# Two token groups in the expert stage of a MetaFormer block: scattered rows, plain loads, an early join

## The reference, cut to what matters

```python
x = x + _L0_conv_ref(_ln_c(x), ...)          # spectral filter, 16 images of 16x16 pixels, 128 channels
t = _to_tokens(x)                             # 4096 tokens of 128 features
t = t + _L0_ffn_ref(_ln_t(t), gate_w, w1, w3, w2)

def _L0_ffn_ref(x, gate_w, w1, w3, w2):       # 8 experts, the best 2 per token, hidden size 384
    gate_logits = xf @ gate_w.T
    weights, indices = jax.lax.top_k(gate_logits, TOP_K)
    weights = jax.nn.softmax(weights, axis=-1)
    for e in range(E):
        h = jax.nn.silu(xf @ w1[e].T) * (xf @ w3[e].T)
        y = h @ w2[e].T
        out = out + combine[:, e:e + 1] * y
```

## Time and profile before

| what | us |
|---|---|
| median of 3 runs (lowest to highest) | 434.74 (433.69 to 437.81) |
| profiled execution, its own time | 437.45 |
| its span, first to last instruction | 435.7 |
| busy in the span: PE, DVE, ACT, POOL | 359.9, 228.7, 166.6, 232.8 |

### The profile page before, as it was taken

The page is one execution under the profiler, slowest core; times in us unless marked ns, Lnnn a source line. Parts: engine busy times, 40 slices in busy tenths (PEclk is TensorE's granted clock), DMA queues, the critical chain, the costliest instruction groups (busy, mean ns, idle before and its releaser), DMA issues.

```text
span 435.7 us, 7026 instructions
## 1 busy us (share of the span) xinstructions
PE 359.9 (83%) x2198; PEld 288.6 (66%) x2198; DVE 228.7 (52%) x556; ACT 166.6 (38%) x326; POOL 232.8 (53%) x255
## 2 busy tenths in 40 slices
PE   1999999963999999859946999999999989989500
PEld 0666666322588888745635999988888888878500
DVE  3376544363479999934972444443334334333147
ACT  2445544322132322145303545444334344434146
POOL 3374342434776555410017577777777777777600
PEclk9999999995899999977955999999999999999955
DMA  7950000035212331571001111111111111112178
GB/s 243 268 127 2 2 0 0 2 84 114 56 42 72 92 90 60 182 257 70 0 6 49 38 54 51 55 50 51 53 56 48 53 52 48 56 50 56 47 260 321
DMA packets 16934, 35.04 MB, mean 80 GB/s; under 512 B 4468, under 2 KB 6152, under 8 KB 16392
## 3 DMA queue, kind: packets, MB, share of 16 engines
q1 hardware_dynamic: 11048, 24.94, 18.6%
q0 software_dynamic: 4544, 9.32, 6.8%
q10 hardware_dynamic: 1312, 0.40, 0.6%
HBM read 21.02 MB, written 9.37 MB: 70 GB/s over the span
## 4 chain that ended last, share of the span: by engine, by line
PE 47%; POOL 23%; issue 10%; DMA 9%; DVE 8%; ACT 2%; SPq 1%; ACTq 0%; POOLq 0%; DVEq 0%
POOL shared L597 11%; POOL y_dram L602 11%; PE psum L823 8%; PE psum L1034 6%; PE psum L912 4%; PE psum L804 3%; PE psum L812 3%; PE psum L1018 3%; PE psum L973 3%; PE psum L888 3%; DMA shared<-tn_dram,idx_gather 2%; PE psum L937 2%; DVE xn L1076 2%; DMA rwc<-in_rwc 2%; PE psum L1009 2%
## 5 line engine op out<-in xcount | busy, mean ns | idle before, releaser
L597 POOL DMA_INDIRECT shared<-tn_dram,idx_gather x71 | 69.0, 972 | 58.7 <-DVE idx_gather L1318 37.3
L602 POOL DMA_INDIRECT y_dram<-shared,idx_scatter x71 | 70.1, 987 | 26.2 <-issue 19.8
L754 ACT ACTIVATE shared<-psum 128x384 f32<-128x384 f32 x71 | 34.8, 491 | 51.5 <-PE psum L1034 50.9
L1034 PE MATMUL psum<-RS,xgt_hl 128*128 x142 | 52.4, 369 | 0.7 <-issue 0.6
L1034 PE MATMUL psum<-w_hi,xgt_hl 128*128 x142 | 48.7, 343 | 0.0
L1076 DVE TENSOR_SCALAR xn<-T,mv,rstd 128x128 f32<-128x128 f32 (+1 forms) x64 | 41.5, 734 | 5.4 <-POOL rstd L510 5.4
L1336 DVE COPY shared<-psum 128x256 f32<-128x256 f32 (+1 forms) x36 | 15.2, 421 | 54.8 <-PE psum L1001 49.9
L1034 PE MATMUL psum<-w_lo,xgt_hl 128*128 x142 | 36.9, 341 | 0.0
L749 ACT ACTIVATE xgt_hl<-psum 128x256 fp32r<-128x256 f32 (+1 forms) x36 | 13.7, 381 | 56.4 <-PE psum L1001 56.4
L1329 DVE TENSOR_TENSOR shared<-shared,psum 128x384 f32<-128x384 f32 x36 | 20.0, 554 | 27.5 <-ACT shared L754 27.5
L823 PE MATMUL psum<-xp,sp 128*64 128x256 f32 x288 | 33.7, 388 | 0.0
(11 more groups left out here) (180 smaller groups left out, 731.8 us busy)
## 6 DMA issues: line engine op xcount, KB each, us to landing
star<-y_dram SPq DMA_DIRECT2D x16, 256.0 KB, 5.6
star<-in_w SPq DMA_DIRECT2D x2, 1536.0 KB, 8.9
rw<-spec SPq DMA_DIRECT2D x8, 256.0 KB, 3.5
turned_b<-spec SPq DMA_DIRECT2D x8, 256.0 KB, 3.6
tn_dram<-xn SPq DMA_DIRECT2D x8, 256.0 KB, 2.1
out<-T SPq DMA_DIRECT2D x8, 256.0 KB, 3.4
spec<-in_w SPq DMA_DIRECT2D x1, 1536.0 KB, 6.6
shared<-in_sp_even SPq DMA_DIRECT2D x1, 1280.0 KB, 15.0
```

The costliest lines, as they stand in the source:

```text
L597: pool.indirect_dma_start(xg[j % BUFS], None, tn_dram, bass.IndirectOffsetOnAxis(ap=idx_gather[:, j:j + 1], axis=0)).then_inc(S[f"g_x{j % ...
L602: pool.indirect_dma_start(y_dram, bass.IndirectOffsetOnAxis(ap=idx_scatter[:, j:j + 1], axis=0), yo[:, j % BUFS * P:j % BUFS * P + P], Non ...
L754: act.activation(silu[j % 2], p_h1[j % 2][:, 0:HID], ACT.Silu).then_inc(S["f_silu"], 1)
L1034: mm = pe.matmul(h[:, 0:HID], xgt[j // 2 % 2][xs][:, j % 2 * P:j % 2 * P + P], w_hl[ws][:, cols], start=(n == 0), stop=(n == 2))
```

## The change

The tokens are cut into two groups: pairs 0 to 3 and pairs 4 to 7. Every expert has a region of rows in DRAM for each group, large enough for all tokens of the group (`xs_dram`), so a token's row can be sent there as soon as its place within the expert is known.

- A row has 130 floats: 128 features, the token's number and its best expert. ACT writes it (`normalise_tokens`, in place of DVE's), with a shift and a scale that POOL makes.
- DVE chooses the experts of group 0 in two halves, at the end of steps 3 and 5 (`choose`: the 11 operations of `top_two` and two copies), places them in steps 4 and 6 (`place`) and makes the tables of the loop (`tables`, 15 operations). PE ranks them with f16 matmuls (`rank`: 9, 17 and, for group 1, 17).
- POOL scatters the rows (`dispatch`), two per token tile: 4 in each of steps 4 to 7, 16 after the last step, all group 0; 8 of group 1 before the loop and 2 in each of its steps 2 to 13.
- From step 4 on the spatial products of the next pair (5, 6, 7) are DVE's instead of POOL's. The step loop is written out.
- w1 and w3 are loaded in the second stage; their splits, the last turns and gatings are interleaved.
- The loop has 39 tiles a group, 78 in all, 40 steps. SP loads each tile as one block whose first row it reads from a table (`load`). Pads of 128 rows mark the ends of the regions; those of group 1 are written between the loads of tiles 7 and 8. DVE makes the scatter addresses from the two extra columns (`slots`, two operations a step).
- Group 0's results are loaded in steps 28 and 34 and joined by DVE in steps 27 to 36 (`join`, 4 operations in each of 8 steps); its pairs are stored before the end. The last four pairs are joined as before.

```diff
+GROUPS = 2
+G_PAIRS = PAIRS // GROUPS
+G_TILES = TILES // GROUPS
 BUFS = 8
-STEPS = (RUN_TILES + 1) // 2
+ROW = DIM + 2
+REGION = G_TILES * P + P
+G_ROWS = E * REGION + E * P
+G_RUN = (2 * G_TILES * P + E * (P - 1)) // P
+G_STEPS = (G_RUN + 1) // 2
+G_SLOTS = 2 * G_STEPS
+STEPS = GROUPS * G_STEPS
-GROUPS = 4
-EARLY = 4 * (PAIRS - 3)
+LATE = PAIRS - 3
+PART_LOAD = G_STEPS + 8
+JOIN_AT = (G_STEPS + 7, G_STEPS + 9, G_STEPS + 13, G_STEPS + 15)
...
+            def pads(g):
+                sp.wait_ge(S["q_tables"], g + 1)
+                for e in range(E):
+                    sp.reg_load(row_reg, pad_at[0:1, g * E + e:g * E + e + 1])
+                    row = sp.snap(row_reg, min_val=0, max_val=GROUPS * G_ROWS - P)
+                    sp.dma_start(xs_dram[ds(row, P), :], io["pads"][e * P:(e + 1) * P, :]).then_inc(S[f"pad_in{g}"], 16)
+            def load(j):
+                wait_step(sp, x_low_done, (j - BUFS) // 2)
+                sp.reg_load(row_reg, tile_rows[0:1, j:j + 1])
+                row = sp.snap(row_reg, min_val=0, max_val=GROUPS * G_ROWS - P)
+                sp.dma_start(xg_all[:, j % BUFS, :], xs_dram[ds(row, P), :]).then_inc(S[f"g_x{j % BUFS}"], 16)
...
+            sp.wait_ge(S["pad_far"], 16 * GROUPS)
+            sp.wait_ge(S["pad_in0"], 16 * E)
+            sp.wait_ge(S["d_out0"], 16 * 2 * G_TILES)
+            for q in range(STEPS):
+                if q == BUFS // 2:
+                    pads(1)
+                if q == G_STEPS:
+                    sp.wait_ge(S["pad_in1"], 16 * E)
+                    sp.wait_ge(S["d_out1"], 16 * 2 * G_TILES)
+                for j in tiles(q):
+                    load(j)
+                if q == PART_LOAD:
+                    results_out(G_RUN - 1)
+                    for i in range(2):
+                        load_results(i)
+                if q == PART_LOAD + 6:
+                    for i in range(2, G_PAIRS):
+                        sp.wait_ge(S["c_done"], i - 1)
+                        load_results(i)
...
+            def inv_std_tokens(i, u):
+                wait_done(pool, S["b_norm"], i - 1)
+                wait_apart(pool, S["b_aggr"], i + 1)
+                pool.tensor_scalar(shift[:, u, :], mv[:, u, :, 0], -1.0, None, ALU.mult)
+                inv_std("b_aggr", "b_eps", "b_rstd", LN_T_EPS, i, u)
+                wait_apart(pool, S["b_rstd"], i + 1)
+                pool.tensor_tensor(shift[:, u, :], shift[:, u, :], rstd[:, u, :], ALU.mult).then_inc(S["b_shift"], 1)
+            def dispatch(n, batch):
+                pool.wait_ge(S["q_place"], batch + 1)
+                for m in range(n):
+                    g, t, k = next(places)
+                    pool.indirect_dma_start(xs_dram, bass.IndirectOffsetOnAxis(ap=idx_dispatch[:, g, k, t:t + 1], axis=0),
+                                            XR[:, g * G_PAIRS + t // 4, t % 4, :], None).then_inc(S[f"d_out{g}"], 16)
+            places = ((g, t, k) for g in range(GROUPS) for t in range(G_TILES) for k in range(2))
             def phase_b(i, u):
-                if not last(i, PAIRS):
+                if i + 1 < LATE:
                     spatial(i + 1, 1 - u)
-                if not first(i):
-                    inv_std("b_aggr", "b_eps", "b_rstd", LN_T_EPS, i - 1, 1 - u)
-                if not last(i, PAIRS):
+                if i > 0:
+                    inv_std_tokens(i - 1, 1 - u)
+                if i + 1 < PAIRS:
                     spectral(i + 1, 1 - u)
+                if i >= 4:
+                    dispatch(4, 0)
+            dispatch(8, 2)
+            for p in range(2, STEPS + 2):
+                for j in tiles(p - 2):
+                    scatter(j)
+                if p < 14:
+                    dispatch(2, 2)
...
+            def normalise_tokens(i, u):
+                if i == 0:
+                    act.wait_ge(S["q_token"], 1)
+                act.wait_ge(S["b_shift"], i + 1)
+                for t in range(4):
+                    op = act.activation(XR[:, i, t, 0:DIM], T[:, 4 * i + t, :], ACT.Identity,
+                                        bias=shift[:, u, t:t + 1], scale=rstd[:, u, t:t + 1])
+                op.then_inc(S["b_norm"], 1)
+            def phase_b(i, u):
+                if i + 1 < LATE:
+                    spatial(i + 1)
+                if i == PAIRS - 1:
+                    weight_high(0)
+                branch_copy(i, u, 0)
+                if i >= 2:
+                    gate_copy(i - 2, u)
+                branch_copy(i, u, 1)
+                if i > 0:
+                    normalise_tokens(i - 1, 1 - u)
...
+            def rank(batch, g, t0, t1, i):
+                pe.wait_ge(S["q_tri"], 3)
+                pe.wait_ge(S["q_count"], batch + 1)
+                pe.wait_ge(S["b_t"], i)
+                n = t1 - t0
+                out = rank_at(n + 1)
+                for t in range(t1):
+                    at = max(t - t0, 0)
+                    pe.matmul(out[:, at:n + 1, :], ones[:, :], q_cnt[:, g * G_TILES + t, :].unsqueeze(1).to_broadcast(
+                        [P, n + 1 - at, E]), start=(t == 0), stop=False)
+                pe.matmul(out[:, 0:n, :], tri[:, :], q_cnt[:, g * G_TILES + t0:g * G_TILES + t1, :], start=False, stop=True)\
+                    .then_inc(S["q_rank"], 1)
+                if i == 4:
+                    rank(0, 0, 0, G_TILES // 2, i)
+                if i == 6:
+                    rank(1, 0, G_TILES // 2, G_TILES, i)
...
+            def spatial(i, u):
+                for j in range(2):
+                    dve.wait_ge(S["b_w"], i * 6 + j + 1)
+                    wait_done(dve, S["b_vt"], i * 2 - 2)
+                    dve.tensor_tensor(u_c[u][j], star_at(j, i), ps_w[j][:, :], ALU.mult).then_inc(S["b_ud"], 1)
...
+            def place(batch, g, t0, t1):
+                n = t1 - t0
+                dve.wait_ge(S["q_rank"], batch + 1)
+                then(dve.tensor_tensor(by_tile(q_slot, n), rank_at(n + 1)[:, 0:n, :], over_tiles(q_first[g], n), ALU.add))
+                then(dve.tensor_tensor(q_sel[:, 0:2 * n * E].rearrange("p (k t e) -> p k t e", k=2, e=E),
+                                       q_oh[:, 0:2 * n * E].rearrange("p (k t e) -> p k t e", k=2, e=E),
+                                       by_tile(q_slot, n).unsqueeze(1).to_broadcast([P, 2, n, E]), ALU.mult))
+                then(dve.tensor_reduce(q_pos[:, 0:2 * n], q_sel[:, 0:2 * n * E].rearrange("p (n e) -> p n e", e=E), AX.X, ALU.add))
+                dve.tensor_copy(idx_dispatch[:, g, :, t0:t1], q_pos[:, 0:2 * n].rearrange("p (k t) -> p k t", k=2))\
+                    .then_inc(S["q_place"], 1)
+            def tables(g):
+                total = rank_at(G_TILES // (2 - g) + 1)[:, G_TILES // (2 - g), :]
+                then(dve.tensor_tensor(pad_at[0:1, g * E:(g + 1) * E], total[0:1, :], q_first[g][0:1, :], ALU.add))
+                then(dve.tensor_scalar(q_e32[:, :], total, float(P - 1), None, ALU.add))
+                dve.tensor_scalar(q_e32[:, :], q_e32[:, :], 7, 7, ALU.logical_shift_right, ALU.logical_shift_left)                    .then_inc(S["q_read"], 1)
+                dve.wait_ge(S["q_read"], g + 1)
...
             def phase_b(i, u):
-                if not last(i, PAIRS):
+                if i + 1 >= LATE and i + 1 < PAIRS:
+                    spatial(i + 1, 1 - u)
+                if i + 1 < PAIRS:
                     filter_products(i + 1, 1 - u, 0)
-                if not first(i):
+                if i > 0:
                     residual(i - 1, 1 - u)
-                if not last(i, PAIRS):
+                if i + 1 < PAIRS:
                     filter_products(i + 1, 1 - u, 1)
-                else:
-                    dve.wait_ge(S["q_iota"], 8 + BUFS)
-                    dve.wait_ge(S["b_logit"], PAIRS - 3)
-                    top_two(0, EARLY)
-                if not first(i):
-                    normalise_tokens(i - 1, 1 - u)
-                if not isinstance(i, int) or 2 <= i < PAIRS - 1:
+                if i == 4:
+                    place(0, 0, 0, G_TILES // 2)
+                if i == 6:
+                    place(1, 0, G_TILES // 2, G_TILES)
+                    tables(0)
+                if i >= 2:
                     logit_copy(i - 2, u)
+                if i in (3, 5):
+                    dve.wait_ge(S["q_iota"], 6 + BUFS)
+                    dve.wait_ge(S["b_logit"], i - 1)
+                    choose((i - 3) * 4, (i - 1) * 4)
...
+            def slots(q):
+                g = slice(tiles(q)[0], tiles(q)[-1] + 1)
+                b = slice(2 * q % BUFS, 2 * q % BUFS + len(tiles(q)))
+                other = q_pos[:, 2 * q % G_TILES:2 * q % G_TILES + len(tiles(q))]
+                then(dve.tensor_tensor(other, xg_all[:, b, DIM + 1], q_expert[:, g], ALU.not_equal))
+                dve.scalar_tensor_tensor(out=idx_scatter[:, g], in0=other, scalar=float(NTOK),
+                                         in1=xg_all[:, b, DIM], op0=ALU.mult, op1=ALU.add)
...
+            def join(i, t):
```

(47 more changed lines are left out.)

454 lines of the change are left out of this document (198 added, 256 removed).

## The result

| | median us (lowest to highest) | profiled execution | its span |
|---|---|---|---|
| before | 435.66 (433.69 to 437.81), 4 runs | 437.45 | 435.7 |
| changed | 414.50 (413.91 to 415.63), 4 runs | 415.63 | 413.9 |

The ratio is 0.9516, 95% interval 0.9462 to 0.9571: faster. 414 was forecast. The profiled executions differ by 21.8 us, where the sum of the steps gave 20.9.

What follows compares the result with a forecast made beforehand. Loop bound by POOL's indirect transfers, its start by PE's wait for routing, the end by transfers and join. Terms -11.9 + 0.3 - 3.8 - 5.5 = -20.9 us from the 434.74 median give 413.8, forecast 414; range 409 to 421.

Steps and rivals of the forecast that it cites:

- The loop: Expert loop with its first loads: -18.9 + 15.1 = -3.8 us for rate and extra tiles, +0.3 us for loads.
- The 18.9 us of POOL's bound: Expert loop: POOL's indirect transfers cost 18.9 us over 26 steps, which go once two scatters a step remain.
- POOL's backlog of group 1's rows: Loop steps 2 to 13: POOL falls 10 us behind, the output buffer covers 12.4; nothing counted, +4 as a bound.
- the first loads: Loop start: SP's loads and pad blocks land tile 9 at 233.9, PE wants tile 8 then: +0.3 us.
- the rival built on slower loads: Loop start: SP's register loads take twice PE's, the first loads stall PE by 5 us: 419 us, chance 0.10.
- The start: Start of the expert loop: first expert matmul at 222.3 instead of 234.2, -11.9 us.
- the 3.5 forecast: Second stage: removed work, PE's waits for choosing and rank matmuls sum to 3.5 us later (-3.3 + 3 + 3.8).
- The end: After the last scatter: with half the pairs joined in the loop, 15.7 us against 21.2, -5.5 us.
- 3 x 2.34 more: End: the four remaining pairs arrive 2.34 us apart, three such distances after the first.
- the slow case: Rival: row transfers of 520 bytes cost 2.0 us each instead of 1.27, slower than before: 450 us, chance 0.08.
- Steps of the loop: Rival: scatter-row operations on PE's path lengthen 39 loop steps by 0.4 us, 15.6 in all: 430 us, chance 0.12.
- the rival that DVE is held by POOL: Second stage: DVE's new small operations double in time beside POOL, +8 us: 422 us, chance 0.15.

Runs made afterwards that it cites:

- e5: The kernel before with the loop's gathers taken off POOL, SP reading each tile by a plain transfer at a fixed address; 413.56 us, ratio 0.9436.
- e9: The changed kernel with group 1's pad blocks issued one a step instead of eight in a row ahead of tile 8; 413.57 us.
- e1: The changed kernel with pair 5's spatial product back on POOL and step 6's choosing behind the spatial product and first filter products; 412.78 us.
- e2: The changed kernel with only POOL's row transfers moved: 4, 5, 5, 2 + 1 in steps 4 to 7 instead of 4 in each; 412.65 us.
- e6: The changed kernel with the sums of pairs 6 and 7 moved from POOL to DVE and the row transfers moved up; 407.31 us.
- e4: The changed kernel with the early join undone, all eight pairs read back and joined after the last scatter; 421.62 us.
- e3: The changed kernel with the loop's loads waiting for eight more row transfers, those of the second group; 424.66 us.

## Why the prediction was right, and where its terms were off

*The loop: right.* -3.6 us measured, -3.5 forecast (-3.8 and +0.3). The 18.9 us of POOL's bound are shown by e5 (19.4). POOL's backlog of group 1's rows stopped nobody: PE is full over the switch of groups, 17.00 of 17.00 us. The term inside that was too small is the first loads, 0.9 us for 0.3 (e9), and the working behind that 0.3 gives nothing at all: tile 9 lands at 233.9 in it and is wanted at 233.9. The 19.4 us that e5 shows for 18.9 make up for most of it, so the match of the sum is in part luck. The prediction read the SP queue by 0.94 us a piece; a load took 6.13/8 = 0.77, a pad block 8.03/8 = 1.0, and the loop started earlier relative to them than I had it. SP's register loads, for which only PE had a row:

```profile
L499 SPq TENSOR_LOAD <-tile_rows x78: 261/267/534, 217.3 to 369.0; - x78
```

0.27 us in the median. The Trainium skill, page "DMA: Bandwidth & Descriptors", section "Latency and other measured facts", has a floor of about 600 ns; these 78 loads disagree, and the rival built on slower loads fell with it.

*The start: 222.3 forecast, 223.4 measured,* as a sum of errors that cancel. The last statistics on DVE ended 4.2 us later than before (192.14 against 187.9), near the 3.5 forecast, but out of other parts. The waits of PE for DVE's spatial product were 1.97 and 2.64 us where I took 1.5 each, and behind the second PE's clock was granted at 0.67 in the mean, 1.4 us more. The rank matmuls cost 0.37 and 0.63 us where I had 3.8 in all: the price of the earlier trace rows came from matmuls whose weight loads took 148 ns in the median, these take 98, and issue at a fifth of the distance (0.49 us for sixteen, 0.03 each, for 0.145). Here are PE's two waits, the slow group behind the second, and the ranks of step 4:

```profile
150.26 1.10 PE L963 MATMUL psum<-RS,coef 128*128 128x512 f32 x2 [1.97 <-DVE shared L1280]
...
154.04 0.37 PE L1032 MATMUL psum<-r,ones 128*128 128x72 f16 x8
...
171.51 1.09 PE L963 MATMUL psum<-RS,coef 128*128 128x512 f32 x2 [2.64 <-DVE shared L1280]
172.44 0.60 PE L984 MATMUL psum<-ident,shared 128*128 128x128 f32 x4
172.88 3.35 PE L990 MATMUL psum<-inv,shared 128*128 128x256 f32 x8
```

What I did not carry into the sum is POOL's own queue: step 7's fourth transfer, at 192.42, stood ahead of the last statistics, which began at 193.45 and not 192.2. I had counted POOL's work as "about what a step lasts" and then let it wait for DVE at every step's end; e1, e2 and e6 show that it was all but full from its first transfer on. The sixteenth transfer began at 214.95, 2.5 us after the forecast 212.5. Against these 2.5 us stood SP and PE, which were 1.5 us faster from the sixteenth's landing to the first matmul than the rows of the gathers gave.

```profile
192.42 0.96 POOL L644 DMA_INDIRECT xs_dram<-images,idx_dispatch  x1 [0.30 <-DVE mv L1163]
193.45 0.24 POOL L634 TENSOR_SCALAR shift<-mv 128x4 f32<-128x4 f32 x1
...
195.55 1.10 POOL L644 DMA_INDIRECT xs_dram<-images,idx_dispatch  x1 [0.17 <-issue]
```

*The end: -7.4 us for -5.5, the largest miss.* The term that was mis-sized is "3 x 2.34 more", the distance of four pairs: the first pair was in 3.4 us after the landing, the second 2.3 later, and the other two before DVE asked for them. DVE bounds the rest at 1.6 us a pair, so the three distances took 5.5 us and not 7.0. The rows of the kernel before say the same: the distance of its first three pairs was no rate to carry on, for there too DVE went on from the third pair at 1.60 us, without a wait:

```profile
422.94 0.88 DVE L1374 SCALAR_TENSOR_TENSOR T<-star,mix,T 128x128 f32<-128x128 f32 x3 [0.73 <-DMA star<-y_dram]
...
424.54 0.87 DVE L1374 SCALAR_TENSOR_TENSOR T<-star,mix,T 128x128 f32<-128x128 f32 x3
```

That eight loads are under way now and sixteen were before isn't shown to matter: e5, with all sixteen, has 2.64 us between its first two pairs and 1.59 behind them. e4 confirms the whole step: undone it costs 7.1 us by the median, 6.5 in the traces. The rows of the changed kernel:

```profile
403.56 0.88 DVE L1478 SCALAR_TENSOR_TENSOR T<-star,mix,T 128x128 f32<-128x128 f32 x3 [7.17 <-DMA star<-y_dram]
...
405.83 0.88 DVE L1478 SCALAR_TENSOR_TENSOR T<-star,mix,T 128x128 f32<-128x128 f32 x3 [1.19 <-DMA star<-y_dram]
...
409.02 0.87 DVE L1478 SCALAR_TENSOR_TENSOR T<-star,mix,T 128x128 f32<-128x128 f32 x3
...
410.01 1.28 DVE L1488 TENSOR_TENSOR T<-T,star 128x512 f32<-128x512 f32 x2
```

*The rivals.* Row transfers of 520 bytes cost what gathers cost (954 ns at least, 978 in the mean, 0.30 between them), so the slow case is out. Steps of the loop stayed at 4.32 us. DVE was slower beside POOL at few operations (below), some 2.3 us in all, 1.0 of it in the wait of 2.64. One of the two supports of the rival that DVE is held by POOL was misread: the two operations of the earlier trace rows are of different lines, and in the same trace the small operation of line 1356, of the size of the first, took 0.20 us during the next gather, as long as the first took without one.

*The whole.* That 414 lies so near the median is in part luck: the start came 1.1 us later and the end 1.9 us earlier than forecast.

## What to carry to other kernels

Once an engine's queue holds work from a first event to the one that counts, add up its work and its idle time between the two: what other engines gain in between arrives only as far as it closes that idle time (e1), and every transfer of the queue that the event has to wait for in addition is paid in full (e3). Taking work off it then moves the bound to the next queue quickly (4.4 of 6 to 7 us in e6), so look at what stands there in program order that nobody needs yet. And a distance between arrivals is a price only as far as somebody waits for them: before, the first pairs of the join were 2.27 and 2.41 us apart, but from the third pair on DVE's 1.60 us set the pace, and in the changed kernel from the second.

## What the runs showed of the hardware that was not expected

A short wait of PE can cost more than itself. The work from the two filters behind the wait to the ranks took 3.78 us in e2's step 6, at a granted clock of 1.00 (2.4 GHz), after a wait of 1.99 us. In e2's step 4, after 1.97 us, and in the changed kernel's step 6, after 2.64 us, it took 5.14 us at 0.67 in the mean, part of it at 1.2 GHz: 1.4 us more. The changed kernel's own step 4, after 1.97 us, took 3.78 us at 1.00. Why the one wait is followed by it and the other, as long, is not, the runs don't tell. The busy tables of the changed kernel and of e2:

```profile
171.51:176.65 5.14, 5.05 (x19) 3.87 (x19) 4.16 (x13) 0.38 (x1) 2.59 (x5) 0.67 0.08 28
```

```profile
148.84:153.98 5.14, 5.04 (x19) 4.02 (x19) 4.16 (x13) 0.16 (x1) 1.18 (x3) 0.67 0.71 246
171.12:174.90 3.78, 3.68 (x19) 2.88 (x20) 3.71 (x13) 0.48 (x1) 2.37 (x3) 1.00 0.17 55
```

A DVE operation can be held until POOL's tensor operation is over. In the changed kernel the comparison of logits with their maximum began at 166.97 and took 1.24 us (0.23 for the same line at 169.60): it ended with POOL's sums, which ran from 165.62 to 168.14. So did the same line at 146.40, held for 0.57 us until 146.97 (sums until 146.88), and a cast at 179.00, 0.80 us until 179.80 (sums until 179.78); line 1341 at 178.01, beside the same sums, took 0.63 us where it took 0.29 in step 4. The Trainium skill, page "Advanced Engine Details and Errata", section "VectorE Performance Modes", says that GpSimd and VectorE's two-port operations block each other; the times agree with a block. Not every operation is held: the reduction at 166.72 took its 0.22 us beside the same sums, the two spatial products at 157.82, which read PSUM, the 1.28 us that they take without POOL, and the operations of choosing from 168.50 on, beside row transfers and not sums, 0.17 to 0.23. The held ones here read and write SBUF alone; what decides it the rows don't tell.

```profile
165.62 2.52 POOL L629 TENSOR_TENSOR shared<-shared 128x512 f32<-128x512 f32 x2
```

```profile
166.72 0.22 DVE L1323 TENSOR_REDUCE r<-logits 128x8 f32<-128x64 f32 x1
166.97 1.24 DVE L1324 TENSOR_TENSOR xn<-logits,r 128x64 f32<-128x64 f32 x1
...
169.60 0.23 DVE L1324 TENSOR_TENSOR xn<-xn,r 128x64 f32<-128x64 f32 x1
```
